# Tanh layer of a graph network: expansion in fp32 without a three-part split, and the products as stationary operand of the contraction

## The reference, cut to what matters

```
xs = concat(x[src, :8], x[dst, :8])                    # 16 scalars per edge
xv = concat(x[src, 8:], x[dst, 8:])  as 16 x 3         # 16 vectors per edge
h  = sqrt(2) * relu(emb @ W1 / sqrt(10))               # 16 numbers per edge
w  = (h @ W2 / 4).reshape(E, 7, 16, 8)                 # seven 16 x 8 matrices per edge
s_out = c * (xs . w0 + (xv . y1) . w1)                 # 8 numbers
g_out = c * (xs . w2 + (xv . y1) . w3)                 # 8 numbers
v_out = c' * (xs . w4 (x) y1 + xv . w5 + (xv y2) . w6) # 8 vectors
message = concat(1.593 tanh(s_out), 1.593 tanh(g_out) * v_out) * weight
result  = sum of the messages over the edges that end in a node
```

## Time and profile before

| | |
|---|---|
| median of 3 runs | 14886.34 us (14883.05 to 14889.52) |
| the profiled execution | 14891.23 us |
| its span, first to last instruction | 14889.4 us |
| busy in the span | PE 79%, weight loads 61%, DVE 87%, ACT 53%, POOL 67% |
| mean granted clock of TensorE | 0.888 |

### The profile page before, as it was taken

One profiled execution on the slowest core, in us unless ns is written; L12 is line 12 of the kernel. 1 busy time (PEld: TensorE's weight loads), 2 busy tenths in 40 slices (PEclk: granted clock), 3 DMA queues, 4 the chain that ended last, 5 costly groups with the idle time before them and its releaser, 6 DMA issues. The chain is left out here.

```text
span 14889.4 us, 427370 instructions
## 1 busy us (share of the span) xinstructions
PE 11746.5 (79%) x109342; PEld 9054.7 (61%) x109342; DVE 12928.2 (87%) x30182; ACT 7888.3 (53%) x23572; POOL 9996.3 (67%) x10549
## 2 busy tenths in 40 slices
PE   1555555555548999999999999979788888888888
PEld 1444444444446666666666666667666666666666
DVE  5777777777768999999999999977799999999997
ACT  0555555555536666666666666638344444444443
POOL 4777777777756666666666666638577777777775
PEclk8666666666669999999999999979899999999999
DMA  3555555555542222222222222238211111111111
GB/s 94 84 87 87 86 87 86 87 87 87 87 67 38 36 36 36 36 36 36 36 36 36 36 36 36 36 116 293 57 24 24 24 24 24 24 24 24 24 24 23
DMA packets 2705891, 840.21 MB, mean 56 GB/s; under 512 B 2232498, under 2 KB 2650073, under 8 KB 2704124
## 3 DMA queue, kind: packets, MB, share of 16 engines
q1 hardware_dynamic: 2212179, 616.76, 20.7%
q0 software_dynamic: 312320, 178.52, 9.2%
q10 hardware_dynamic: 181250, 43.25, 1.3%
HBM read 610.22 MB, written 226.58 MB: 56 GB/s over the span
## 5 line engine op out<-in xcount | busy, mean ns | idle before, releaser
L1352 POOL DMA_INDIRECT w_rows<-table,w_idx x9375 | 8929.7, 952 | 4086.9 <-issue 2387.3
L1583 PE MATMUL w_p_w<-w_w,w_ht 128*128 128x256 f32 x12500 | 3007.2, 388 | 125.1 <-DVE w_prodv L1527 124.5
L1335 PE MATMUL w_p_deg<-w_hot_lo,w_hot_row 128*128 128x196 bf16 x6250 | 1797.5, 336 | 1573.4 <-DVE w_hot_lo L1280 1535.0
L1583 PEld LDWEIGHTS w_p_w<-w_w,w_ht 128*128 128x128 f32 x12500 | 2273.1, 190 | 673.5 <-issue 299.4
L1147 ACT ACTIVATE w_dist<-row_iota,w_negrel 128x32 f32<-128x32 f32 x9375 | 2182.6, 315 | 300.1 <-issue 272.2
L1554 ACT ACTIVATE w_ht<-w_p_h 128x512 f32<-128x512 f32 x1875 | 851.2, 526 | 2489.6 <-PE w_p_h L1574 2489.6
L1793 DVE TENSOR_TENSOR w_prod<-w_p_xe,w_he 128x512 f32<-128x512 f32 x3125 | 2137.5, 684 | 4.3 <-PE w_p_xe L1936 4.3
L1309 ACT CAST w_counts<-w_p_count 128x784 uint8<-128x784 f32 x1875 | 1247.2, 706 | 1453.3 <-PE w_p_count L1336 1435.9
L1335 PEld LDWEIGHTS w_p_deg<-w_hot_lo,w_hot_row 128*128 128x128 bf16 x6250 | 829.9, 133 | 1698.1 <-issue 1607.8
L1336 PE MATMUL w_p_count<-w_hot_lo,w_hot_row 128*128 128x196 bf16 x6250 | 1808.6, 336 | 0.0
L1959 PE MATMUL w_p_sgt<-w_prod,w_wc 128*32 128x128 f32 x25000 | 1331.6, 284 | 85.9 <-ACT w_sgt L1872 65.7
(11 more groups left out here) (211 smaller groups left out, 20273.9 us busy)
## 6 DMA issues: line engine op xcount, KB each, us to landing
counts<-w_counts SPq DMA_DIRECT2D x1250, 122.5 KB
d_small<-counts SPq DMA_DIRECT2D x388, 392.0 KB
w_rows<-table,w_idx POOLq DMA_INDIRECT x9375
w_rel_row<-rel_row SPq DMA_DIRECT2D x625, 120.0 KB
w_edge<-e SPq DMA_DIRECT2D x625, 80.0 KB
w_idx<-src SPq DMA_DIRECT2D x1875, 2.5 KB
w_negrel<-negrel SPq DMA_DIRECT2D x1875, 2.5 KB
w_nodes<-split SPq DMA_DIRECT2D x1875, 2.0 KB
```

Source lines behind the costliest of these rows:

```text
L1335: nc.tensor.matmul(p_deg[:], hot_row[s2][:, b, :], hot_lo[s2][:, b, :], start=False, stop=False, skip_group_check=True)
L1352: pool.indirect_dma_start(out=rows[:, t, :], out_offset=None, in_=table[0:N, :], in_offset=bass.IndirectOffsetOnAxis(ap=idx[:, t:t + 1], a ...
L1583: last = nc.tensor.matmul(p_w[(g.base * len(BANKS) + bank) % WBANKS][:, (t - t0) * 256:(t - t0 + 1) * 256], ht[g.slot(UNROLL)][:, k, t * P ...
```

## The change

In the Tanh layer the three-part split is left out. `x32` itself, in fp32, is turned by five fp32 matmuls with the identity; tile t is written to partitions 32 (t mod 4) onwards, tiles 0 to 3 in one block of 128 columns and tile 4 in a second. The expansion takes the 32 rows of its tile and a fp32 0/1 matrix `pick_c` that stands on all four blocks of 32 partitions. In the contraction the operands swap places: `prod` (128 columns) is stationary and `wc` (24 columns) moves, and the four matmuls of a tile add up in `p_out`, with the edge on the partition. `p_sgt`, its copies, `sgt`, `stack` and the stack product go. ScalarE takes tanh from `p_out` once all five tiles are there, and copies the other 8 numbers to a new tile `along`, which VectorE reads in place of `p_out`. The gather product and the hidden layer move ahead of contract 0 in TensorE's order.

```diff
-    SGT, G_ROWS, T_AT, QUAD, WIDE = 24, 16, 16, 32, 64
+    OUT, G_ROWS, T_AT = 24, 16, 16
-        p_out = p_low[:, T * D + WIN:T * (D + WIDE) + WIN].rearrange("p (t o) -> p t o", o=WIDE)
-        p_sgt = ps("p_sgt", [P, 4 * P])
-        p_he = ps("p_he", [P, 1024])
-        p_xt = p_he[0:SPLIT * 32, :]
+        p_out = ps("p_out", [P, T, OUT])
+        p_he = ps("p_he", [P, GE + 2 * P])
+        p_xt = p_he[:, GE:GE + 2 * P].rearrange("p (r e) -> p r e", e=P)
...
-        xs = [sb(f"xs{s}", [P, T, SPLIT, 32], BF16) for s in range(2)]
-        rest = [sb(f"rest{s}", [P, T, 32]) for s in range(2)]
-        xt = [sb(f"xt{s}", [P, GE], BF16) for s in range(2)]
+        xt = [sb(f"xt{s}", [P, 2, P]) for s in range(2)]
-        sgt = [sb(f"sgt{s}", [P, GE]) for s in range(2)]
-        stack = sb("stack", [P, WIDE])
+        along = [sb(f"along{s}", [P, T, 8]) for s in range(2)]
-        wc = sb("wc", [P, 4, QUAD])
+        wc = sb("wc", [P, 4, OUT])
-        pick_f = sb("pick_f", [SPLIT * 32, 4, P])
-        pick_b = sb("pick_b", [P, 4, P], BF16)
+        pick_c = sb("pick_c", [P, 4, P])
...
@@ POOL, setup: 16 selects in place of 12
-                for part in range(SPLIT):
+                for q in range(4):
...
@@ VectorE
-                    vec.tensor_sub(rest[s2][:], x32[s2][:], xs[s2][:, :, 0, :]).then_inc(rest_ready, 1)
-                    vec.tensor_sub(xs[s2][:, :, 2, :], rest[s2][:], xs[s2][:, :, 1, :]).then_inc(low_ready, 1)
-                    done(dve, bent_ready, g)
+                    done(dve, along_ready, g)
-                    ... spread(p_out[:, :, T_AT:SGT], [P, T, 8, 3], 3),
+                    ... spread(along[s2][:], [P, T, 8, 3], 3),
...
@@ ScalarE
-                if g := at(4):
-                    activate(g, 4, T)
-                if g := at(2):
-                    nc.scalar.copy(xs[s2][:, :, 0, :], x32[s2][:]).then_inc(high_ready, 1)
+                if g := at(4):
+                    act.wait_ge(tile_out, g.times(T, T))
+                    free(act, gate_ready, g, 2)
+                    free(act, vout_ready, g, 2)
+                    nc.scalar.activation(bent[s2][:], p_out[:, :, 0:G_ROWS], ACT.Tanh, scale=1.0 / 32 ** 0.5).then_inc(bent_ready, 1)
+                    nc.scalar.copy(along[s2][:], p_out[:, :, T_AT:OUT]).then_inc(along_ready, 1)
...
-                    done(act, out_ready, g)
-                    nc.scalar.activation(bent[s2][:], p_out[:, :, 0:G_ROWS], ACT.Tanh, scale=1.0 / 32 ** 0.5).then_inc(bent_ready, 1)
-                    nc.scalar.copy(xs[s2][:, :, 1, :], rest[s2][:]).then_inc(mid_ready, 1)
-                    nc.scalar.copy(xt[g.slot(2)][0:SPLIT * 32, :], p_xt[:, 0:GE]).then_inc(xt_ready, 1)
-                if g := at(3):
-                    free(act, out_ready, g, 2)
-                    activate(g, 0, 4)
+                    nc.scalar.copy(xt[s2][:, 0, :], p_xt[:, 0, :])
+                    nc.scalar.copy(xt[s2][0:32, 1, :], p_xt[0:32, 1, :]).then_inc(xt_ready, 1)
...
@@ TensorE, expand
+                rows = slice(t % 4 * 32, t % 4 * 32 + 32)
-                    last = nc.tensor.matmul(p_xe[b][:, i * P:(i + 1) * P], pick_b[:, i, :], xt[g.slot(2)][:, t * P:(t + 1) * P],
+                    last = nc.tensor.matmul(p_xe[b][:, i * P:(i + 1) * P], pick_c[rows, i, :], xt[g.slot(2)][rows, t // 4, :],
                                             start=True, stop=True)
@@ TensorE, contract
                 pe.wait_ge(prod_ready, g.times(T, t + 1))
                 if t == 0:
-                    free(pe, sgt_last, g, 1)
-                if t == 4:
-                    done(pe, sgt_first, g)
+                    free(pe, bent_ready, g, 1)
+                    free(pe, along_ready, g, 1)
                 for i in range(4):
-                    last = nc.tensor.matmul(p_sgt[QUAD * i:QUAD * (i + 1), t % 4 * P:(t % 4 + 1) * P], wc[:, i, :], prod[b][:, i, :],
-                                            start=True, stop=True)
+                    last = nc.tensor.matmul(p_out[:, t, :], prod[b][:, i, :], wc[:, i, :], start=i == 0, stop=i == 3)
@@ TensorE, step
-                if g := at(4):
-                    done(pe, sgt_last, g)
-                    ...
-                    for t in range(T):
-                        last = nc.tensor.matmul(p_out[:, t, :], sgt[g.slot(2)][:, t * P:(t + 1) * P], stack[:],
-                                                start=True, stop=True)
-                    last.then_inc(out_ready, 1)
-                if g := at(3):
-                    contract(g, 0)
-                    expand(g, 2)
-                    vector_weights(g, 0, 1)
                 if g := at(1):
...
                     wg.product(pe, g)
...
                 if g := at(3):
+                    contract(g, 0)
+                    expand(g, 2)
+                    vector_weights(g, 0, 1)
                     contract(g, 1)
...
-                    for e in range(T):
-                        last = nc.tensor.matmul(p_xt[:, e * P:(e + 1) * P], xs[g.slot(2)][:, e, :, :].rearrange("p s i -> p (s i)"),
-                                                ident_b[:], start=True, stop=True)
+                    for t in range(T):
+                        last = nc.tensor.matmul(p_xt[t % 4 * 32:t % 4 * 32 + 32, t // 4, :], x32[g.slot(2)][:, t, :], a["ident"][:], start=True, stop=True)
```

More of the change, by code:

```diff
@@ L1723, in _ @@
         def _(pool):
[L1725 removed]
+            pool.memset(pick_c[:], 0.0).then_inc(picks, 1)
             for b in range(4):
[L1727 to L1730 removed]
+                for q in range(4):
+                    pool.wait_ge(picks, 4 * b + q + 1)
+                    view = pick_c[:, b, :].rearrange("p (u h) -> p u h", h=HID1)
+                    pool.affine_select(out=view, in_=view, compare_op=ALU.not_equal, fill=1.0, base=-(32 * q + 8 * b),
                                        pattern=[[-1, 8], [0, HID1]], channel_multiplier=1).then_inc(picks, 1)
@@ L1791, in tile_products @@
                 dve.wait_ge(xe_ready, g.times(T, t + 1))
-                wait_count(dve, sgt_tile, g.times(T, t - 1))
+                wait_count(dve, tile_out, g.times(T, t - 1))
                 vec.tensor_mul(prod[b][:], p_xe[b][:].rearrange("p (i e) -> p i e", e=P),
@@ L1811, in step @@
                     done(dve, dots_ready, g)
-                    free(dve, low_ready, g, 2)
+                    free(dve, xt_mm, g, 2)
                     vec.tensor_reduce(x32[g.slot(2)][:, :, 16:32], dots[g.slot(2)][:], AX.X, ALU.add).then_inc(q_ready, 1)
@@ L1815, in step @@
                     tile_products(g, 1)
-                if g := at(2):
-                    s2 = g.slot(2)
-                    done(dve, high_ready, g)
-                    free(dve, low_ready, g, 2)
-                    vec.tensor_sub(rest[s2][:], x32[s2][:], xs[s2][:, :, 0, :]).then_inc(rest_ready, 1)
                 if g := at(4):
                     s, s2 = g.slot(UNROLL), g.slot(2)
-                    done(dve, bent_ready, g)
+                    done(dve, along_ready, g)
                     free(dve, redv_ready, g, 1)
-                    vec.tensor_mul(prodv[:].rearrange("p t (k w u) -> p t w k u", k=3, w=8)[:, :, :, :, 8], spread(p_out[:, :, T_AT:SGT], [P, T, 8, 3], 3),
+                    vec.tensor_mul(prodv[:].rearrange("p t (k w u) -> p t w k u", k=3, w=8)[:, :, :, :, 8], spread(along[s2][:], [P, T, 8, 3], 3),
                                    spread(unit[s][:], [P, T, 8, 3], 2)).then_inc(vout_ready, 1)
@@ L1867, in _ @@
         def _(act):
-            def activate(g, t0, t1):
-                act.wait_ge(sgt_tile, g.times(T, t1))
-                at, n = t0 % 4 * P, (t1 - t0) * P
-                nc.scalar.copy(sgt[g.slot(2)][:, t0 * P:t1 * P], p_sgt[:, at:at + n]).then_inc(sgt_last if t1 == T else sgt_first, 1)
             def step(at):
                 if g := at(4):
-                    activate(g, 4, T)
-                if g := at(2):
                     s2 = g.slot(2)
-                    done(act, q_ready, g)
-                    free(act, xt_mm, g, 2)
-                    nc.scalar.copy(xs[s2][:, :, 0, :], x32[s2][:]).then_inc(high_ready, 1)
+                    act.wait_ge(tile_out, g.times(T, T))
[3 more added lines that the diff above has]
+                    nc.scalar.copy(along[s2][:], p_out[:, :, T_AT:OUT]).then_inc(along_ready, 1)
                 if g := at(1):
@@ L1885, in step @@
                     arrived(act, gathered, g, GATHERED)
-                    free(act, low_ready, g, 2)
+                    free(act, xt_mm, g, 2)
                     free(act, wv_used, g, UNROLL)
@@ L1974, in step @@
                     expand(g, 1)
-                if g := at(4):
-                    done(pe, sgt_last, g)
-                    pe.wait_ge(dst_copied, g.times(1, 3) if at(2) else G)
-                    free(pe, w.acc_added, g, 1)
-                    for t in range(T):
-                        last = nc.tensor.matmul(p_out[:, t, :], sgt[g.slot(2)][:, t * P:(t + 1) * P], stack[:],
```

(9 more changed lines are left out.)

41 lines of the change are left out of this document (11 added, 30 removed).

## The result

The changed kernel takes 25,109.46 us (median of four runs, 25,104.69 to 25,115.55) against 14,885.82 us: 1.687 times as long (95% interval 1.684 to 1.690), 10,224 us more. That is outside the forecast's own range (17,190 to 18,690), inside the wider one that was meant to leave out no more than 2 in 10 (17,050 to 25,500), and where the rival "the clock falls" put it (24,400 to 25,900 us).

What follows compares the result with a forecast made beforehand. VectorE set the 8.42 us period before; TensorE would become the only bound at 13.67 us per group, so (13.67 - 8.42) x 625 = 3,280 us more: 18,170 us, range 17,190 to 18,690, chance of full clock 0.54.

Steps and rivals of the forecast that it cites:

- the clock falls: Rival, Tanh layer: TensorE drops to 1.2 GHz, 24,400 to 25,900 us; chance 0.30 for part or all of the layer.
- the wait at L1826: VectorE's product waiting for ScalarE's tanh, 0.37 us per group; said to shrink as the stack product leaves its chain.
- The sum at full clock: TensorE's work per group in the Tanh layer at 2.4 GHz: 12.10 us without row-shape changes, 13.67 with them and bare loads.
- Ten row-shape changes and four bare first loads: TensorE, around the 32-row expansions: ten changes at 0.12 us, 1.2 us, and bare loads 0.37 us per group.
- the prediction's own price of 0.058 per 128: TensorE: a bf16 matmul of 128 columns costs 0.058 us, read from four expansion matmuls in 0.23 us.
- VectorE's work: VectorE in the Tanh layer: 7.4 us per group after losing two subtractions worth 0.63 us.
- the final sums: Last layer's fp32 bursts on 64 rows at clock 0.51, TensorE busy 16 of 20 us: sign for the falling clock.
- still stream 128 columns and more: Sign against the falling clock: vector weights, hidden layer and expansion stream wide between contractions of 0.9 us.
- that rival: Loads don't overlap in the 32-row expansion: 4.3 us more, 18 us per group, 20,860 us; chance 0.06.

Runs made afterwards that it cites:

- experiment 5: All-row version with: one tile on 32 rows 22,818.03 us; 96 rows 17,127.14; 64 rows 25,115.94; tiny extra matmuls on 32 rows 17,859.22, on 128 rows 17,277.61.
- the push: Changed kernel plus 40 fp32 matmuls of 128 rows and 512 columns, once, early in the layer: 25,148.97 us.
- experiment 4: Kernel before with one part alone: the new fp32 expansion on 32 rows 23,272.02 us; the new contraction 19,256.3 us, with 160 extra bf16 matmuls once 19,251.92 us.
- experiment 1: Changed kernel with the expansion on all 128 rows, its 0/1 matrices zero on other tiles' rows: 17,166.67 us.
- experiment 2: Changed kernel with the contraction's weights and p_out padded with zeros from 24 to 96 columns: 24,617.41 us.

## Why the prediction was wrong

**What held.** TensorE becomes the only bound; VectorE falls idle, waiting for the expansion; the wait at L1826 goes; nothing else comes late (TensorE is busy 4,000 of 4,000 us). The counts (40 records for each part) are right. The sum at full clock is right as well: 12.10 us without row-shape changes, 12.01 measured with 96 or 128 rows. Some of that is luck: expansion and contraction together take 1.79 us a tile, as predicted, but the one measured 0.97 (predicted 0.90) and the other 0.82 (0.89).

**What was mis-sized in the sum.** Ten row-shape changes and four bare first loads stood in it with 1.57 us. (The 0.12 us per change was read with 0.53 us for 1,280 bf16 columns; by the prediction's own price of 0.058 per 128 they are 0.58, which leaves 0.07.) The extra matmuls of experiment 5 measured 0.97 us for ten. The changed kernel itself, in the two expansions behind the push, took 0.50 us more than on 128 rows for four changes with the loads behind them, so 1.25 for ten. With these a group is 12.98 to 13.26 us, and the time at full clock, had the chip granted it, 14,891 + (12.98 to 13.26 - 8.42) x 625 = 17,740 to 17,920 us, an estimate, 250 to 430 below the forecast. VectorE's work was put too low: 7.4 us a group in the prediction, 8.0 measured (1,285.79 in 161 groups); it took the two subtractions at their drawn 0.63 us, while drawn times of instructions that follow each other at once overlap (those of VectorE before add up to 4,395 us, in 3,806 of busy time). None of that made the prediction wrong.

**The step that failed** is the weighing of "the clock falls" at 0.30 (0.20 for the whole layer) against 0.54 for full clock. For it stood the final sums: fp32 bursts on 64 rows at 0.51 with TensorE drawn busy in 16 of 20 us. That row mixes two things. Finer stretches of that time in the kernel before, and a line of TensorE's timeline:

```profile
9760.00:9762.00 2.00, 0.19 (x2) 0.06 (x1) 1.48 (x3) 0.46 (x2) 0.00 (x0) 0.60 0.00 0
9766.00:9796.00 30.00, 30.00 (x132) 30.00 (x132) 18.35 (x22) 0.00 (x0) 0.00 (x0) 0.50 0.00 1
```
```profile
9763.42 1.78 PE L1159 MATMUL w_p_low<-w_hot,w_msg 128*96 128x32 f32 x10 [3.22 <-DVE w_msg L1856]
```

The clock fell while TensorE stood idle, before the first of the bursts on 64 rows (9,765.84 us); these then ran without a gap at 0.50. So the rows didn't show such bursts losing the clock, they showed them not raising it, with TensorE drawn busy throughout. Against the rival the prediction set that vector weights, hidden layer and expansion "still stream 128 columns and more". The expansion was on the wrong side of that sentence: it streams 128 columns, but on 32 rows, and experiment 4 gave 0.50 with it alone. The sentence fails without the 32 rows as well: with the contraction alone, the bursts between the contractions (vector weights, hidden layer, bf16 expansion) streamed 128 columns and more on 128 rows, and the clock was 0.50, too. The size of the rival was right: 23.6 to 26 us per group, 24.8 measured.

**The cause**, as far as the runs show it: in the changed kernel it is the expansion on 32 rows (experiment 1 gives 1.00 back with the same number of instructions, 96 rows do too); not a cold start (the push), not the changes of shape (experiment 5), not the narrow contraction alone in this place (experiment 2). The contraction has the same fault of its own: with the bf16 expansion beside it, it loses the clock too, while beside the full-row fp32 expansion it doesn't. What the chip counts stays open; the runs say only which of these kernels kept the clock. Open, too, is what lifts it: the kernels on all rows reached 1.00 at 4,503, 4,539 and 4,583 us (the two of experiment 5 with the extra matmul, changes of shape first, and experiment 1), and with one tile on 32 rows the same bursts on 128 rows stayed at 0.50.

**The rules cited.** The Trainium skill, "TensorE: Matmul & The Clock Gate", Part 1 (What's actually happening), says that the gate follows how busy the PE has been. Here TensorE is drawn busy 4,000 of 4,000 us at 0.50, and as fully busy with 96 rows at 1.00: the drawn busy share doesn't tell the clock, the measurement decides. The Trainium skill, same page, Part 3 (The mechanism), has in one of its sentences that loads overlap only when the row group differs; a record of the expansion took 0.208 us at 1.2 GHz in one 32-row group, load and stream overlapped, so that rival falls. The Trainium skill, "TensorEngine Tiling (Array Packing)", Tiling Modes, lists 64 and 32 rows as modes of their own and says that a change of mode drains the engine: the runs fit that, with 0.097 us per change between 128 and 32 rows and nothing for 96; they don't show the drain itself.

## What to carry to other kernels

A burst that uses 32 or 64 of the array's rows isn't cheaper by its rows, and it can cost the whole stage half of TensorE's clock: try 96 or 128 rows, with zeros in the stationary operand, before anything else (here 25,109 to 17,127 us, though still 2,240 above the kernel before). Before an operand swap or a smaller shape goes into a stage that needs TensorE at full clock, look for a stretch in the trace with bursts of that shape, and take its granted clock as the first guess, even where other bursts lie between; whether these hold the clock has to be tried (the contraction ran at 0.50 beside bf16 expansions, at 1.00 beside fp32 ones on 128 rows). A busy share of 100% says nothing on the clock; read the two columns together.

## What the runs showed of the hardware

- In this kernel 96 rows behave as 128 (next burst after 0.97 us, clock 1.00), 64 as 32 (25,116 and 25,109 us, clock 0.50).
- One tile of five on 32 rows was enough to bring the layer to a mean of 0.56, with a rise and a fall in each group, while ten changes of shape per group with next to no work in the small shape left it at 1.00.
- A push brings 1.00 in both kernels that were pushed. In the changed one it was gone about 5 us after the push (4,758 to 4,763 us), in the one with the contraction alone after some 43 us.
- Rows whose weights are all zero were enough: the version on all rows adds only such rows to the expansion, and it ran at 1.00 (17,167 us).
- TensorE drawn busy without a gap can stay at 0.50: over 4,000 us in the changed kernel, over 30 us in the final sums before it.
